# Attention values and softmax sums for four heads at a time, in 32-column groups

## What is computed

```python
# per sequence; H = 16 heads of DH = 64
x  = x + attention(layernorm(x))
    # sim = 50 * tanh(q k^T / 8 / 50), causal mask, softmax, out = attn v, then Wo
x  = x + ffn(layernorm(x))
    # shared = gelu(t sw1 + sb1) sw2 + sb2
    # router: softmax over 8 experts, best 2 kept with their probabilities
    # routed = sum over the 2 of p * (gelu(t w1[e] + b1[e]) w2[e] + b2[e])
```

## Time and profile before

| | us |
|---|---|
| median of 3 runs | 2106.31 (2105.99 to 2106.75) |
| the profiled execution, whole | 2105.01 |
| its span on the core | 2102.2 |
| TensorE busy | 1975.4 (94%) |
| VectorE busy | 1697.7 (81%) |
| ScalarE busy | 1417.6 (67%) |
| GpSimd busy | 1037.6 (49%) |
| mean granted TensorE clock | 0.982 |

### The profile page before, as it was taken

One profiled execution on the slowest core, in us unless ns is written; L12 is line 12 of the kernel. 1 busy time (PEld: TensorE's weight loads), 2 busy tenths in 40 slices (PEclk: granted clock), 3 DMA queues, 4 the chain that ended last, 5 costly groups with the idle time before them and its releaser, 6 DMA issues.

```text
span 2102.2 us, 35982 instructions
## 1 busy us (share of the span) xinstructions
PE 1975.4 (94%) x12605; PEld 1557.8 (74%) x12605; DVE 1697.7 (81%) x2867; ACT 1417.6 (67%) x2170; POOL 1037.6 (49%) x1204
## 2 busy tenths in 40 slices
PE   6899999999999999999999999999999783999998
PEld 4577777777777777777777777777777562999998
DVE  6678888888888888888888888898988886565565
ACT  6678686868686868686868686868686651444444
POOL 3435454545454545454555555554545453344344
PEclk9999999999999999999999999999999996999999
DMA  4000101010101010101010101010101024764664
GB/s 130 1 21 1 51 1 51 1 51 1 51 1 51 1 51 1 51 1 51 1 51 1 51 1 51 1 51 1 51 1 41 1 71 128 227 190 134 190 183 140
DMA packets 73649, 112.24 MB, mean 53 GB/s; under 512 B 9716, under 2 KB 52219, under 8 KB 73477
## 3 DMA queue, kind: packets, MB, share of 16 engines
q1 hardware_dynamic: 58468, 67.86, 11.4%
q0 software_dynamic: 15008, 42.10, 5.4%
HBM read 63.10 MB, written 48.65 MB: 53 GB/s over the span
## 4 chain that ended last, share of the span: by engine, by line
PE 72%; DVE 15%; ACT 8%; issue 3%; DMA 1%; POOL 0%; SPq 0%; POOLq 0%; DVEq 0%
PE bank_o L1181 10%; PE ring L1161 6%; PE ring L1140 6%; PE ring L1088 5%; PE ring L1166 5%; PE ring L1089 5%; PE ring L1094 5%; DVE norm L766 3%; ACT prob L557 3%; PE bank_d L1192 3%; PE ring L1147 3%; ACT prob L563 2%; PE acc L1201 2%; DVE kT L752 2%; DVE q_lo L757 2%
## 5 line engine op out<-in xcount | busy, mean ns | idle before, releaser
L557 ACT ACTIVATE prob<-ring 128x1024 f32<-128x1024 f32 (+1 forms) x384 | 327.0, 877 | 223.3 <-PE ring L1166 219.6
L766 DVE RECIPROCAL norm<-bank_d 128x512 f32<-128x512 f32 x128 | 429.5, 3356 | 26.8 <-PE bank_d L1192 25.0
L483 POOL TENSOR_SCALAR_AFFINE_SELECT prob<-prob 128x256 f32<-128x256 f32 x512 | 220.0, 450 | 447.5 <-ACT prob L563 447.5
L494 POOL TENSOR_TENSOR key_sum<-prob 128x768 f32<-128x768 f32 x128 | 241.3, 1885 | 345.0 <-PE bank_d L1192 338.2
L563 ACT ACTIVATE prob<-prob 128x1024 f32<-128x1024 f32 (+1 forms) x384 | 344.3, 915 | 5.2
L1181 PE MATMUL bank_o<-prob,v 128*64 128x512 f32 (+3 forms) x2048 | 308.4, 444 | 18.6 <-DVE norm L768 18.6
L752 DVE TENSOR_TENSOR kT<-ring,kT 64x512 fp32r<-64x512 f32 x256 | 176.3, 689 | 124.6 <-ACT kT L570 120.9
L1161 PE MATMUL ring<-qT,kT 128*128 128x256 f32 (+3 forms) x1024 | 239.2, 335 | 32.2 <-DVE xnTl L739 11.8
L1181 PEld LDWEIGHTS bank_o<-prob,v 128*64 128x64 f32 x2048 | 128.2, 138 | 177.3 <-issue 154.9
L1161 PEld LDWEIGHTS ring<-qT,kT 128*128 128x128 f32 x1024 | 165.5, 189 | 110.1 <-issue 50.5
L1166 PE MATMUL ring<-q_lo,kT 128*128 128x256 f32 (+3 forms) x1024 | 225.5, 322 | 0.4 <-DVE q_lo L757 0.4
(11 more groups left out here) (222 smaller groups left out, 4766.6 us busy)
## 6 DMA issues: line engine op xcount, KB each, us to landing
xin<-first SPq DMA_DIRECT2D x71, 257.0 KB, 3.3
xin<-second SPq DMA_DIRECT2D x71, 129.0 KB, 2.7
xin<-base SPq DMA_DIRECT2D x71, 128.0 KB, 2.8
x_next<-in_x SPq DMA_DIRECT2D x16, 512.0 KB, 3.8
x_res<-in_x SPq DMA_DIRECT2D x16, 512.0 KB, 3.8
raw_e<-in_w SPq DMA_DIRECT2D x4, 1024.0 KB, 7.1
first<-pad SPq DMA_DIRECT2D x9, 257.0 KB, 4.8
second<-pad SPq DMA_DIRECT2D x9, 129.0 KB, 5.7
```

The costliest lines, as they stand in the source:

```text
L483: last = nc.gpsimd.affine_select(out=diag, in_=diag, compare_op=ALU.is_ge, fill=0.0, base=0, pattern=[[0, 2], [1, P]], channel_multiplier=-1)
L494: nc.gpsimd.tensor_tensor(key_sum[:, :, :], t0[:, :, P:N], t13[:, :, 0:N - P], ALU.add).then_inc(sum_steps, 1)
L557: nc.scalar.activation(probs[p % 2][u][:, :, :], slot[:, :, 0:UNIT_COLS[u]], ACT.Tanh, scale=SCALE / SOFTCLAMP).then_inc(act_emptied, 1)
L766: nc.vector.reciprocal(norm[:, :], bank_d[:, :]).then_inc(o_steps, 1)
```

## The change

Values are computed in chunks: chunk c of a sequence holds 32 of the 64 dimensions (half c % 2) of the four heads of quad c // 2, each head in its own 32-column group, 16 matmuls in a chunk in place of 8 in a pair. There are eight chunks in a sequence, as there were eight pairs. The denominators are computed once for a quad, in four 32-column groups, and their reciprocal once, with a chunk's even number; both chunks use it. The rows of the output weight are reordered on the host to match. A quad needs the probabilities of two pairs, so there are four `probs` and two `key_sum` buffers.

The order moves too. On TensorE, values of chunk p - 2 run in step p (the last two of a sequence in steps 0 and 1 of the next), denominators at even p, `project_out` is that of chunk p - 4, and two v units each run at p = 1 and 2. On VectorE, chunk p - 3 is handled in step p; the split of an odd chunk stands behind `empty_qk`; chunk 5 of the sequence before falls to step 0, chunks 6 and 7 to step 1; step 2 has none, and the residual and the second layernorm run there. `prepare_bias` moves to p = 3 to 6.

In SBUF `hT` lies in `x2T`, `gelu` beside it, there is one row buffer (two headers around the same normalised row, `fill_row1` falls away), both expert biases share one `b_rows` with a selecting operand `bias_of`, and the padding block `pad` is cleared and made a second time after the last projection.

```diff
@@ -84,8 +93,8 @@
                 units += [(FFN_UNITS[p], i - 1, 0, 0)]
             if i + 1 < NSEQ and p == 6:
                 units += [("turn1", i + 1, 0, 0)]
-            if p == 0:
-                units += [("v", i, t, 0) for t in range(NT)]
+            if p in V_UNITS:
+                units += [("v", i, t, 0) for t in V_UNITS[p]]
 UNIT_ORDER = (2, 0, 1)
+V_UNITS = {1: (0, 1), 2: (2, 3)}
...
             probs = [[sb(f"prob{k}{u}", [P, 2, UNIT_COLS[u]], F32, arena) for u in range(3)]
-                     for k in range(2)]
-            key_sum = sb("key_sum", [P, 2, N - P], F32, arena)
+                     for k in reversed(range(PROBS))][::-1]
+            key_sum = [sb(f"key_sum{k}", [P, 2, N - P], F32, arena) for k in range(2)]
...
             def sum_keys(i, p):
-                t0, t13, t2 = probs[p % 2]
-                if g >= 1:
-                    pool.wait_ge(den_done, g)
+                t0, t13, t2 = probs[p % PROBS]
+                sums = key_sum[p % 2]
+                if g >= 2:
+                    pool.wait_ge(den_done, g // 2)
...
-                    if p == 2 and i >= 1:
-                        fill_row1(i - 1)
             send_first(NSEQ - 2)
-            fill_row1(NSEQ - 1)
+            pool.wait_ge(projected, NSEQ * PAIRS)
+            clear_pad()
+            pool.wait_ge(pad_ready, 3)
+            finish_pad()
...
+                    if p in V_UNITS:
+                        if i >= 1:
+                            act.wait_ge(valued, i * PAIRS)
+                        for t in V_UNITS[p]:
                             copy_v(i, t)
...
-            def normalise(i, p):
-                g = i * PAIRS + p
+            def weigh_values(i, c):
+
+                g, quad = i * PAIRS + c, (i * PAIRS + c) // 2
+                if c % 2 == 0:
+                    if g >= 1:
+                        dve.wait_ge(o_steps, 3 * g)
+                    dve.wait_ge(den_done, quad + 1)
+                    nc.vector.reciprocal(norm[:, :], bank_d[:, :]).then_inc(inverted, 1)
+                    dve.wait_ge(inverted, quad + 1)
+                dve.wait_ge(valued, g + 1)
                 if g >= 1:
-                    dve.wait_ge(o_steps, 4 * g)
-                dve.wait_ge(den_done, g + 1)
-                nc.vector.reciprocal(norm[:, :], bank_d[:, :]).then_inc(o_steps, 1)
-                dve.wait_ge(o_steps, 4 * g + 1)
-                nc.vector.tensor_tensor(norm[:, :], bank_o[:, :], norm[:, :], ALU.mult).then_inc(o_steps, 1)
-                dve.wait_ge(o_steps, 4 * g + 2)
+                    dve.wait_ge(o_steps, 3 * g)
+                nc.vector.tensor_tensor(weighed[:, :], bank_o[:, :], norm[:, :], ALU.mult).then_inc(o_steps, 1)
+
+            def split_values(i, c):
+                g = i * PAIRS + c
+                dve.wait_ge(o_steps, 3 * g + 1)
                 if g >= 1:
                     dve.wait_ge(projected, g)
-                nc.vector.tensor_copy(oT[0][:, :], norm[:, :]).then_inc(o_steps, 1)
-                dve.wait_ge(o_steps, 4 * g + 3)
-                nc.vector.tensor_tensor(oT[1][:, :], norm[:, :], oT[0][:, :].bitcast(F32),
+                nc.vector.tensor_copy(oT[0][:, :], weighed[:, :]).then_inc(o_steps, 1)
+                dve.wait_ge(o_steps, 3 * g + 2)
+                nc.vector.tensor_tensor(oT[1][:, :], weighed[:, :], oT[0][:, :].bitcast(F32),
                                         ALU.subtract).then_inc(o_steps, 1)
...
             for i in range(NSEQ):
                 for p in range(PAIRS):
+
+                    chunk = (i, p - 3) if p >= 3 else (i - 1, p + 5)
+                    if p == 2 or chunk[0] < 0:
+                        chunk = None
                     if i >= 1:
-                        if p == 1:
-                            add_attention(i - 1)
-                            layernorm_guess(2, i - 1)
-                            layernorm_newton(2, i - 1)
                         if p == 5:
                             empty_logits(i - 1)
                         if p == 7:
                             place_tokens(i - 1)
-                    if p >= 2:
-                        normalise(i, p - 2)
-                    if p == 0 and i >= 1:
-                        normalise(i - 1, PAIRS - 2)
+                    if i == 0 and p == 3:
+                        dve.wait_ge(idle_padded, 16 * 3)
+                    if chunk is not None:
+                        weigh_values(*chunk)
+                        if chunk[1] % 2 == 0:
+                            split_values(*chunk)
                     if p + 1 < PAIRS:
                         empty_qk(i, p + 1)
                     elif i + 1 < NSEQ:
                         empty_qk(i + 1, 0)
+                    if chunk is not None and chunk[1] % 2 == 1:
+                        split_values(*chunk)
...
-                    if p == 0:
-                        if i >= 1:
...
+                    if p == 0 and i + 1 < NSEQ:
+                        dve.wait_ge(xnext_loaded, 16 * (i + 2))
+                        layernorm_stats(1, x_next)
+                        layernorm_guess(1, i + 1)
+                        layernorm_newton(1, i + 1)
+                        layernorm_apply(1, i + 1, x_next, x_next, xn_ready)
+                    if p == 1 and i >= 1:
+                        weigh_values(i - 1, PAIRS - 1)
+                        split_values(i - 1, PAIRS - 1)
+                    if i == NSEQ - 1 and p in (3, 4, 5, 6):
+                        prepare_bias(p - 3)
                     if i >= 1:
                         if p == 2:
-                            layernorm_apply(2, i - 1, row0[:, :, 0:D], stream, x2n_ready)
+                            add_attention(i - 1)
+                            layernorm_guess(2, i - 1)
+                            layernorm_newton(2, i - 1)
+                            normalise_rows(i - 1)
...
-            normalise(last_i, PAIRS - 2)
-            normalise(last_i, PAIRS - 1)
+            for c in range(PAIRS - 3, PAIRS):
+                weigh_values(last_i, c)
+                split_values(last_i, c)
...
-            def values(i, p):
-                g = i * PAIRS + p
+            def values(i, c):
+
+                g, quad, half = i * PAIRS + c, c // 2, c % 2
                 if g >= 1:
-                    pe.wait_ge(o_steps, 4 * g - 2)
+                    pe.wait_ge(o_steps, 3 * (g - 1) + 1)
                 units = [(u, j, at) for u in range(3) for j, at in SCORE_UNITS[u]]
-                if p == 0:
+                if c == 0:
                     pe.wait_ge(act_emptied, EMPTIED[AT["v", i, NT - 1, 0]][0])
-                pe.wait_ge(masked, 3 * g + 3)
+                pe.wait_ge(masked, 3 * (i * PAIRS + 2 * quad + 1) + 3)
                 for k, (u, j, at) in enumerate(units):
-                    for h in range(2):
-                        f = p * P + h * DH
-                        pe.matmul(bank_o[h * DH:(h + 1) * DH, j * P:N], v[:, j, f:f + DH],
-                                  probs[p % 2][u][:, h, at:at + N - j * P],
-                                  start=(k == 0), stop=(k == len(units) - 1))
+                    for h in range(QUAD):
+                        f = (quad * QUAD + h) * DH + half * QD
+                        last = pe.matmul(bank_o[h * QD:(h + 1) * QD, j * P:N], v[:, j, f:f + QD],
+                                         probs[(2 * quad + h // 2) % PROBS][u][:, h % 2, at:at + N - j * P],
+                                         start=(k == 0), stop=(k == len(units) - 1))
+                last.then_inc(valued, 1)
+
+            def denominators(i, quad):
+                g = i * PAIRS // 2 + quad
+                if g >= 1:
+                    pe.wait_ge(inverted, g)
+                for h in range(QUAD):
+                    pe.matmul(bank_d[h * QD:(h + 1) * QD, 0:P], ones[:, 0:QD],
+                              probs[(2 * quad + h // 2) % PROBS][0][:, h % 2, 0:P], start=True, stop=True)
+                pe.wait_ge(sum_steps, 3 * (2 * g + 1) + 3)
+                for h in range(QUAD):
...
-                    if p >= 3:
-                        project_out(i, p - 3)
-                    if p == 0 and i >= 1:
-                        project_out(i - 1, PAIRS - 3)
+                    if p >= 4:
+                        project_out(i, p - 4)
+                    elif i >= 1 and p < 2:
+                        project_out(i - 1, p + 4)
+                    elif i >= 1 and p == 2:
+                        project_out(i - 1, PAIRS - 1)
...
-                    if p >= 1:
-                        values(i, p - 1)
-                        denominators(i, p - 1)
-                    if p == 0:
+                    if p == 1:
                         if i >= 1:
                             values(i - 1, PAIRS - 1)
-                            denominators(i - 1, PAIRS - 1)
                         else:
                             pe.wait_ge(lo_split, 3)
                         project_v(i, 0)
```

(39 more changed lines are left out.)

172 lines of the change are left out of this document (85 added, 87 removed).

## The result

Before 2106.53 us, after **2222.59 us** (medians of four runs each, 2105.99 to 2107.23 and 2221.03 to 2224.02); ratio 1.055 (95% interval 1.053 to 1.057). The direction was forecast, the size was not: +116 against +52, and outside the range. The waits that were forecast can be found in the trace; the largest of them is 5.9 us and not 3.4, and the last sequence loses twice what it was given. Beside the experiments the kernel before took 2102.9 to 2110.5 us in single executions, a spread of 0.4% and not of under 0.1%, and one slow execution of 3248 us at a granted clock of 0.56 is left out.

The account below looks back on a forecast made before the run. TensorE's order and waits bound the kernel (72% of the chain). From 2105.0 us, +32 for waits less denominators, +17 clock, -2 first and +6 last sequence give 2158 profiled, 2159 us as median; range 2120 to 2195.

Parts of the forecast that it names:

- +2.3 of waits less denominators: Middle sequence: 105.56 us less 3.84 of denominators, plus waits of 3.4, 1.25, 1.3 and 0.25, gives 107.9 us.
- Values 2.20 a chunk, whether four groups run side by side: TensorE's values: a chunk takes 2.20 us if four column groups run side by side, 4.4 if only two do.
- The rival with two abreast: Four column groups don't run side by side: a chunk takes 4.4 us, the kernel about 2420 us; chance 0.06.
- the estimate of 2.7: Chunk time in us by the skill's speedup for 32-column groups, 0.5 more than 2.20; the prediction doubted so much.
- Wait in stage 1, 3.4 us (2.9 to 4.2): TensorE waits before chunk 7's values until VectorE has weighed chunk 6, behind layernorm and reciprocal; 14 of 16 sequences.
- Clock, 1.6 us in three sequences of four: TensorE's clock falls to 0.50 behind the stage 1 wait; +17 us in all, bounds 0 and 46.
- Copy of v's last tile, 1.25 us: End of stage 2: TensorE waits 1.25 us before chunk 0's values for ScalarE's copy of v 3.
- Stage 3 at 10.4, ScalarE: Stage 3 lasts 10.4 us, as the next scores need ScalarE's last copy of q; 1.3 us more.
- 0.25 for the small rest: Stage 6 gives back some 0.15 us and bank waits in stages 1 to 3 come out 0.1 longer.
- First sequence -2: First sequence: two v units now precede the values that waited 9.11 us; -2 us, bounds -10 and +3.
- Last sequence +6 for the bias preparations: Last sequence: four 6.3 us preparations moved to stages 3 to 6 can hold up TensorE; +6 us, bounds 0 and +15.
- The rival "TensorE's work alone": If VectorE finishes layernorm and reciprocal before TensorE asks, only work counts: 2045 us, up to 2070; chance 0.16.

Follow-up runs that it names:

- experiment 2: Changed kernel with GpSimd's key sums of pair 0 moved one stage later, VectorE's order unchanged; 2181.78 us, ratio 1.037.
- experiment 3: Changed kernel with 20 extra 512-column matmuls, their result unused, put before chunk 7's values on TensorE; 2202.03 us, ratio 1.046.
- experiment 11: Changed kernel with layernorm behind chunk 7's weighing, stage 3's last exponential later, bias preparations spread, plus chunk 0's last key tile taken last; 2110.46 us, ratio 1.003.
- Experiment 12: Kernel of experiment 11 with GpSimd's key sums of pair 2 also waiting for VectorE's layernormed residual rows; 2077.56 us, ratio 0.987.
- experiment 7: Kernel of experiment 1 with ScalarE's last exponential of stage 3 put behind the copies of k and q; 2102.59 us, ratio 0.998.
- experiment 1: Changed kernel with the next sequence's layernorm moved on VectorE behind chunk 7's weighing and split; 2115.09 us, ratio 1.0045.
- experiments 5: Kernel of experiment 1 with quad 0's denominators ahead of chunk 0's values on TensorE; 2171.97 us, ratio 1.031.
- experiment 4: Changed kernel with the first v unit put ahead of chunk 7's values on TensorE in stage 1; 2183.98 us, ratio 1.038.

## Why the prediction was right in direction and wrong in size

For a middle sequence the forecast was +3.5 us (+2.3 of waits less denominators, +1.2 of clock); measured +7.53. In all it fell short by 66 us: 35 by the wait of stage 1, 8 by the clock, 14 by small things in the middle sequences, 3 and 6 by the first and the last. By its steps:

- *Values 2.20 a chunk, whether four groups run side by side.* Right, 2.18. The rival with two abreast is out, and so is the estimate of 2.7 from the Trainium skill ("TensorE: Matmul & The Clock Gate", Part 3): its figure for narrow groups does not hold for these.
- *Wait in stage 1, 3.4 us (2.9 to 4.2).* The place, the releaser and the queue were right, the size was the step that failed: **5.9 us**. The term mis-sized in it is the layernorm, taken at the 5.49 us of the earlier trace rows and in fact 8.05. I took a duration from a place where GpSimd had no key sum to run, and did not ask what GpSimd would be doing at the new one. Experiment 2 takes the key sums away and gets 3.55 us. +2.5 us in each of 14 sequences, 35 us; without them the kernel takes 2182 us, inside the range.
- *Clock, 1.6 us in three sequences of four.* Near in size, in part by luck: 1.75 us (experiment 3), but as the mean of all 14. A stretch at 0.50 begins in each of these waits, 24 us in all, not 17. At a wait of the length that was forecast (experiment 2) there is one in 7 of 14, and stage 1 is 0.94 us longer in the mean than the 19.96 us of those without, where the forecast had 1.2.
- *Copy of v's last tile, 1.25 us.* 1.15; covering it (experiments 11 and 12) gave 1.22.
- *Stage 3 at 10.4, ScalarE.* 10.46, and it was ScalarE (experiment 7).
- *0.25 for the small rest.* Too little. 7.53 + 3.84 - 5.9 - 1.75 - 1.15 - 1.3 leaves 1.3 us. Some 0.65 of it is stage 0, forecast at 10.16 and 10.81 in the mean: its scores wait 0.58 us for the bank that VectorE empties after the stage has begun (L930, 1.29 us at 1029.90). The other 0.6 wasn't traced; it is what is left over.
- *First sequence -2.* +1.4. What there ate the expected gain was not tested; from version to version this sequence took between 101.0 and 106.0 us.
- *Last sequence +6 for the bias preparations.* +11.8, by the mechanism that was forecast, at about twice the size. Three of the four preparations hold TensorE up, for 4.4, 6.5 and 7.2 us (stages 4, 5 and 7), with 6.8 us at 0.50 at each; in the kernel before the waits of 1.9 us and more up to the last scores are 1.9, 3.0 and 6.3. The last of the preparations stands ahead of the copies of the token places, which empty the bank that the last scores need:

```profile
1815.92 2.18 DVE L967 CAST b_rows<-x_next 2x1024 fp32r<-2x1024 f32 x1
...
1821.47 1.30 DVE L974 SCALAR_TENSOR_TENSOR b_rows<-x_next,ident,b_rows 2x1024 fp32r<-2x1024 f32 x1
...
1822.95 0.21 DVE L901 COPY totals_of<-ring 128x64 f32<-128x64 f32 x1
```

```profile
1823.22 1.22 PE L1209 MATMUL ring<-qT,kT 128*128 128x512 f32 x2 [7.19 <-DVE totals_of L901]
...
1827.12 0.52 PE L1253 MATMUL acc<-w_oh,oTh 128*128 128x256 f32 x1
```

  The scores of the last pair begin 106.3 us into the last sequence (107.8 before) and take 11.8 us, 1815.3 to 1827.1, where they took 2.6: 9.2 of the 11.8 us. The preparation was itself drawn out, 6.9 us in all: its copy took 2.18 us beside a key sum and 0.67 in stage 5. A further 3.5 us are the drain: from the end of these scores to the last output projection it is 27.1 us, 23.6 before. A quad is whole only when its second pair is, so two chunks, the denominators and a reciprocal hang behind the last scores. The forecast had no such term; that this is the reason for the 3.5 us is argued and not tested. The 7.2 us wait is in every version here, the fastest too.

The rival "TensorE's work alone" had its condition right: experiment 1 gets the weighing through in time and wins 107 us. It had its price wrong: with the condition met the kernel takes 2115 us and not 2045 to 2070. Experiment 12 covers two waits more. By the traces its span is 34 us longer than the span before less 3.84 us in each of 16 sequences. Of these, 25 lie in the 14 middle sequences (103.49 us each, not 101.71), 4 in the first and 5 in the last. In a middle one it is some 0.6 us of stage 0 and the 0.7 us by which stage 3 is longer than TensorE's 8.99 in it; the rest wasn't traced.

The whole again: wait 14 x 5.9 = 83, clock 24, v's copy, stage 3 and the small rest 14 x 3.75 = 52, ends 13, denominators 14 x -3.84 = -54; sum 118, and 118.9 between the spans. The small rest was found by subtraction, so the sum shows how large the parts are and does not test them.

## What to carry to other kernels

When a change moves an instruction into another stage, its duration from the old place is only good if the other engines do the same beside it: put VectorE's and GpSimd's timelines of the new place over each other before you add up. An edit that makes TensorE earlier also releases GpSimd earlier, and that can land on VectorE: experiments 5 and 11 were right about their own stage and lost 57 and 18 us elsewhere, and one wait on GpSimd turned each into a gain. And walk the last round by itself: work put at the end of one step stands ahead of what the next step begins with, as the bias preparation did ahead of the token places, and work that needs two items instead of one may leave a longer drain.

## What the runs showed of the hardware that was not expected

- VectorE's steps on 128x4 elements, 0.16 to 0.17 us alone, lasted 0.59 to 1.81 us beside GpSimd's key sums, each until 0.02 to 0.03 us after the key sum's end; four steps of 128x256 took 2.92 and not 1.38. The reciprocal (3.35 to 3.36 us) and the differences of q and k (1.39 for two), which read PSUM, took the same beside key sums as without.
- With the 5.9 us wait came 6.8 us at 0.50 in 11 of 14 sequences and 3.4 us in three, beginning 1.9 to 5.3 us into the wait; it cost about half of the part that lay behind the wait (1.75 us of 3.66 in the mean). With waits of about 3.1 us (experiment 4) came a stretch in 12 of 14, with about 3.5 us (experiment 2) in only 7 of 14. In experiment 11 idling of 1.12 us, as in its row, and of 0.51 us 1.3 us later came with a 3.4 us stretch in 9 of 14, while 1.94 us had left the clock up. So the length of one wait alone did not tell whether the clock would drop.
- Four column groups of 32 in fp32 ran side by side as well as two of 64: the 32 matmul records of a chunk in 2.18 us, the 16 of a pair in 2.20.
